# P V products of two key blocks in one group, and projection chunks placed by time, in a fused attention and expert block

## What is computed

```python
xq, xk, xv = x @ wq.T, x @ wk.T, x @ wv.T            # each split into 16 heads
probs = softmax(einsum('bqhd,bkhd->bhqk', xq, xk))   # no scaling
att   = einsum('bhqk,bkhd->bqhd', probs, xv).reshape(4, 1024, 512) @ wo.T
x = layernorm(x + att)
logits = x @ Wr.T + br                               # 8 experts
h = einsum('nd,erd->ner', x, A)                      # all experts, rank 64
y = einsum('ner,eor->neo', h, B) / 64                # the expert of the largest logit, times its softmax
x = layernorm(x + selected y)
```

## Time and profile before

| | us |
|---|---|
| median of 3 timed runs | 1701.31 |
| lowest and highest | 1699.29, 1701.86 |
| the profiled execution | 1692.17 |
| span of its trace | 1690.3 |
| TensorE matmul busy | 1580.4 (94% of the span) |
| GpSimd busy | 1175.7 (70%) |
| VectorE busy | 942.7 (56%) |
| ScalarE busy | 770.5 (46%) |

### The profile page before, as it was taken

The page is one execution under the profiler, slowest core; times in us unless marked ns, Lnnn a source line. Parts: engine busy times, 40 slices in busy tenths (PEclk is TensorE's granted clock), DMA queues, the critical chain, the costliest instruction groups (busy, mean ns, idle before and its releaser), DMA issues.

```text
span 1690.3 us, 19384 instructions
## 1 busy us (share of the span) xinstructions
PE 1580.4 (94%) x6432; PEld 755.5 (45%) x6432; DVE 942.7 (56%) x1688; ACT 770.5 (46%) x1409; POOL 1175.7 (70%) x653
## 2 busy tenths in 40 slices
PE   5979999999999999999999999999999999999897
PEld 2534444444444444444444454444444444444343
DVE  1645556654465566655456555755545676773433
ACT  1144455554445444444444444444544555555322
POOL 1067889987777667667778766686777888889600
PEclk9999999999999999999999999999999999999899
DMA  7343434332032222234331133312423112210001
GB/s 242 95 131 107 151 101 111 103 104 73 10 93 70 76 71 69 56 94 126 94 84 48 40 82 88 82 46 85 141 45 88 45 46 58 57 39 20 7 1 50
DMA packets 82066, 132.08 MB, mean 78 GB/s; under 512 B 18592, under 2 KB 36016, under 8 KB 81968
## 3 DMA queue, kind: packets, MB, share of 16 engines
q1 hardware_dynamic: 78704, 125.59, 26.8%
q0 software_dynamic: 1152, 4.22, 0.7%
q10 hardware_dynamic: 2112, 1.05, 0.2%
HBM read 87.84 MB, written 42.20 MB: 77 GB/s over the span
## 4 chain that ended last, share of the span: by engine, by line
PE 83%; DVE 7%; issue 4%; POOL 3%; ACT 2%; DMA 1%; SPq 1%; ACTq 0%; POOLq 0%
PE sc L547 14%; PE pv L559 13%; PE w L448 13%; PE mx L537 13%; PE w L459 7%; PE w L511 6%; PE w L470 5%; PE w L498 5%; DVE mxc L723 2%; POOL Psum L382 2%; PE w L492 1%; DMA wqk_s<-wkT 1%; DVE eq L804 1%; ACT P L612 1%; PE w L505 1%
## 5 line engine op out<-in xcount | busy, mean ns | idle before, releaser
L723 DVE TENSOR_REDUCE mxc<-mx 128x1 f32<-128x512 f32 x1024 | 685.0, 686 | 589.1 <-PE mx L537 585.9
L382 POOL TENSOR_TENSOR Psum<-Psum,P 128x1024 f32<-128x1024 f32 x384 | 901.9, 2366 | 150.4 <-ACT P L612 146.0
L612 ACT ACTIVATE P<-sc 128x512 f32<-128x512 f32 x1024 | 594.3, 596 | 653.4 <-PE sc L547 644.8
L547 PE MATMUL sc<-stack 98*128 98x512 f32 x1024 | 679.6, 664 | 13.8 <-DMA stack<-mrow 12.0
L537 PE MATMUL mx<-stack 96*128 96x512 f32 x1024 | 412.9, 406 | 6.4 <-DVE mxc L723 6.4
L547 PEld LDWEIGHTS sc<-stack 98*128 98x128 f32 x1024 | 193.4, 189 | 292.5 <-issue 138.5
L378 POOL TENSOR_TENSOR Psum<-P 128x1024 f32<-128x1024 f32 x64 | 151.2, 2369 | 233.5 <-ACT P L612 226.6
L448 PE MATMUL w<-xT_s,wqk_s 128*128 128x512 f32 x512 | 266.6, 613 | 27.2 <-DMA wqk_s<-wkT 17.7
L559 PE MATMUL pv<-P,V 128*32 128x512 f32 x2048 | 273.6, 606 | 0.0
L537 PEld LDWEIGHTS mx<-stack 96*128 96x128 f32 x1024 | 195.5, 191 | 171.8 <-issue 140.8
L448 PEld LDWEIGHTS w<-xT_s,wqk_s 128*128 128x128 f32 x512 | 92.7, 192 | 112.2 <-issue 85.7
(11 more groups left out here) (108 smaller groups left out, 821.6 us busy)
## 6 DMA issues: line engine op xcount, KB each, us to landing
stack<-qk_parts SPq DMA_DIRECT2D x192, 256.0 KB, 5.3
qk_parts<-split SPq DMA_DIRECT2D x64, 512.0 KB, 2.8
xT_s<-xT SPq DMA_DIRECT2D x8, 1024.0 KB, 10.2
den_s<-den_parts SPq DMA_DIRECT2D x124, 64.0 KB, 2.0
r<-x SPq DMA_DIRECT2D x3, 2048.0 KB, 8.6
out<-r SPq DMA_DIRECT2D x12, 512.0 KB, 3.0
wqk_s<-wqT SPq DMA_DIRECT2D x14, 256.0 KB, 4.0
wqk_s<-wkT SPq DMA_DIRECT2D x14, 256.0 KB, 4.3
```

The lines of the kernel that those rows point to most:

```text
L382: pool.tensor_tensor(Psum[:, s % 2, i, :], Psum[:, s % 2, i, :], P[:, unit % NP, :], ALU.add).then_inc(add_done, 1)
L547: pe.matmul(sc[c][:, :], stack(s, i)[0:KS, 0, 128 * kb:128 * kb + 128], stack(s, i)[0:KS, 1, 512 * c:512 * c + 512], start=True, stop=True ...
L612: act.activation(P[:, unit % NP, 512 * c:512 * c + 512], sc[c][:, :], ACT.Exp).then_inc(exp_done, 1)
L723: dve.tensor_reduce(mxc[:, q % 2, m:m + 1], mx[g % NMX][:, :], AX.X, ALU.max).then_inc(mx_done, 1)
```

## The change

Three things are changed.

1. `out_block` becomes `out_group`: the P V matmuls of two key blocks follow one another, eight in a group. There are four groups in a slot: after the max item of h11, h19 and h27, and h3 of the next slot. What waits for `pv_done` counts groups: `exp` of a unit waits for the group that read its P buffer, `copy_v` and `copy_out` likewise. The number of P buffers stays six.
2. The three segments are gone. `paced` walks through the halves with a cost for each (2 for a half, 9 more for a half with a group, 4 for a chunk) and places chunks so that the sum grows evenly. Halves with a group get no chunk, nor mostly does the half behind it. A slot's pieces keep their order.
3. `den` and `max_t` are no longer at fixed halves. They go to the first half from h10 and h26 on in which no piece is half done, and at the latest to h12 and h28 in the middle of a piece. SyncE's `load_max` stands in the half after `max_t`. The steps behind `den` (spread, store, reload, inversion, normalisation) count from h12 instead of h10.

```diff
-    SEGMENTS = ((0, 10), (10, 26), (26, 32))
+    HALF_COST, GROUP_COST = 2, 9
+    DEN_AT, MAX_AT = 10, 26
...
+    def group_of(h):
+        k, c = divmod(h, 2)
+        return k // 4 - 1 if c == 1 and k % 4 == 1 else None
...
+    def paced(pieces, pinned):
+        pieces, pinned = list(pieces), list(pinned)
+        chunks = [(kind, n, c) for kind, n in pieces for c in range(CHUNKS[kind])]
+        cost = [HALF_COST + (GROUP_COST if group_of(h) is not None else 0) for h in range(HALVES)]
+        work = sum(WEIGHT.get(kind, 4) for kind, _, _ in chunks) + sum(WEIGHT[kind] for _, (kind, _) in pinned)
+        each, spent, out = (sum(cost) + work) / HALVES, 0, []
+        for h in range(HALVES):
+            spent += cost[h]
+            out.append([])
+            while pinned and h >= pinned[0][0] and (not chunks or chunks[0][2] == 0 or h >= pinned[0][0] + 2):
+                _, (kind, n) = pinned.pop(0)
+                out[-1].append((kind, n, 0))
+                spent += WEIGHT[kind]
+            while chunks and (h + 1 == HALVES or spent + WEIGHT.get(chunks[0][0], 4) / 2 <= each * (h + 1)):
+                out[-1].append(chunks.pop(0))
+                spent += WEIGHT.get(out[-1][-1][0], 4)
...
         def den_half(s):
-            return HALVES * (s + 1) + SEGMENTS[1][0]
+            return HALVES * (s + 1) + DEN_AT + 2
...
-                if h == SEGMENTS[2][0] + 1 and s < LAST:
-                    load_max(s + 1)
+                for q in ends(half - 1, "max_t"):
+                    load_max(q)
...
-            def out_block(s, kb):
-                pe.wait_ge(exp_done, 2 * (UNITS * s + 2 * kb + 2))
+            def out_group(s, g):
+                pe.wait_ge(exp_done, 2 * (UNITS * s + 4 * g + 4))
...
-                for c in range(2):
-                    for i in range(2):
+                for kb in (2 * g, 2 * g + 1):
+                    for c in range(2):
+                        for i in range(2):
...
-                if c == 1 and k == 1 and s:
-                    out_block(s - 1, KB - 1)
-                if c == 1 and k % 2 == 1 and k >= 3:
-                    out_block(s, (k - 3) // 2)
+                g = group_of(half % HALVES)
+                if g is not None and (g >= 0 or s):
+                    out_group(s if g >= 0 else s - 1, g % GROUPS)
...
-                    act.wait_ge(pv_done, (unit - NP) // 2 + 1)
+                    act.wait_ge(pv_done, (unit - NP) // 4 + 1)
```

More of the change, by code:

```diff
@@ L23, in build_attention_lora_moe_block @@
     KB = S // 128
+    GROUPS = KB // 2
     PAIRS = H // 2
@@ L42, in build_attention_lora_moe_block @@
     CHUNKS = {"qk": KT, "v": KT, "o": KT, "part": KT - 1, "h": KT, "z": KT, "t1": 1, "t2": 1, "lg": 1, "den": 1, "max_t": 1}
-    WEIGHT = {"t1": 2, "t2": 2, "lg": 4, "den": 0, "max_t": 0}
-    SEGMENTS = ((0, 10), (10, 26), (26, 32))
+    WEIGHT = {"t1": 2, "t2": 2, "lg": 4, "den": 4, "max_t": 1}
+    HALF_COST, GROUP_COST = 2, 9
+    DEN_AT, MAX_AT = 10, 26
     def qks(b, first, n):
@@ L104, in build_attention_lora_moe_block @@
     OPENING = qks(0, 0, 4) + tiles("v", 0, 0, 8) + qks(0, 4, 2) + [("max_t", 0)] + qks(0, 6, 2)
+    def group_of(h):
[17 more added lines that the diff above has]
+                spent += WEIGHT.get(out[-1][-1][0], 4)
+                while pinned and h >= pinned[0][0] and (not chunks or chunks[0][2] == 0):
+                    _, (kind, n) = pinned.pop(0)
+                    out[-1].append((kind, n, 0))
+                    spent += WEIGHT[kind]
+        return out
     AT, ENDS = {}, {}
@@ L107, in build_attention_lora_moe_block @@
     for s in range(SLOTS):
[L108 to L119, removed]
+        pinned = ([(DEN_AT, ("den", s - 1))] if s else []) + ([(MAX_AT, ("max_t", s + 1))] if s < LAST else [])
+        for h, chunks in enumerate(paced([piece for part in PLAN[s] for piece in part], pinned)):
+            for kind, n, c in chunks:
+                AT.setdefault(HALVES * s + h, []).append((kind, n, c))
+                if c == 0:
+                    ORDER.append((kind, n))
                 if c + 1 == CHUNKS[kind]:
-                    ENDS.setdefault(half, []).append((kind, n))
-                spent += weight
-            ORDER += pinned + pieces
+                    ENDS.setdefault(HALVES * s + h, []).append((kind, n))
     FIRST = KB * (B - 1)
@@ L348, in _ @@
                 for after, job in ((1, spread_den), (3, store_rec), (4, load_rden)):
-                    if s and h == SEGMENTS[1][0] + after:
+                    if s and half == den_half(s - 1) + after:
                         job(s - 1)
-                if h == SEGMENTS[2][0] + 1 and s < LAST:
-                    load_max(s + 1)
+                for q in ends(half - 1, "max_t"):
+                    load_max(q)
             for g in range(KB // 2):
@@ L548, in score @@
                           stack(s, i)[0:KS, 1, 512 * c:512 * c + 512], start=True, stop=True).then_inc(sc_ready, 1)
-            def out_block(s, kb):
-                pe.wait_ge(exp_done, 2 * (UNITS * s + 2 * kb + 2))
+            def out_group(s, g):
+                pe.wait_ge(exp_done, 2 * (UNITS * s + 4 * g + 4))
                 if s % PAIRS == 0:
-                    pe.wait_ge(v_done, KB * (s // PAIRS) + kb + 1)
-                if kb == 0 and s:
+                    pe.wait_ge(v_done, KB * (s // PAIRS) + 2 * g + 2)
+                if g == 0 and s:
                     pe.wait_ge(pv_copied, s)
-                for c in range(2):
-                    for i in range(2):
[L558 to L561, removed]
+                for kb in (2 * g, 2 * g + 1):
+                    for c in range(2):
+                        for i in range(2):
+                            at, head = HD * (2 * c + i), 2 * (s % PAIRS) + i
+                            done = pe.matmul(pv[at:at + HD, :], V[:, kb, HD * head:HD * head + HD],
+                                             P[:, (UNITS * s + 2 * kb + i) % NP, 512 * c:512 * c + 512],
+                                             start=(kb == 0), stop=(kb == KB - 1))
                 done.then_inc(pv_done, 1)
@@ L587, in _ @@
                     KIND[kind](n, chunk, bank)
-            out_block(LAST, KB - 1)
+            out_group(LAST, GROUPS - 1)
             pe.wait_ge(exp_done, 2 * UNITS * SLOTS)
@@ L622, in copy_v @@
                 if n >= KB:
-                    act.wait_ge(pv_done, KB * (PAIRS * (n // KB) - 1) + n % KB + 1)
+                    act.wait_ge(pv_done, GROUPS * (PAIRS * (n // KB) - 1) + n % KB // 2 + 1)
                 act.activation(V[:, n % KB, :], BANK["v", n][:, :], ACT.Copy).then_inc(v_done, 1)
             def copy_out(s):
-                act.wait_ge(pv_done, KB * (s + 1))
+                act.wait_ge(pv_done, GROUPS * (s + 1))
                 if s > 1:
@@ L859, in _ @@
                     gates(n)
-                if s and h == SEGMENTS[1][0] + 3:
+                if s and half == den_half(s - 1) + 3:
                     reciprocal(s - 1)
```

## The result

The changed kernel takes 1748.19 us (median of 4 runs, 1747.45 to 1750.94), the kernel before, run beside it, 1701.03 us. The ratio is 1.028, with a 95% interval of 1.026 to 1.030. The change makes the kernel 47 us slower, where 1695 us was forecast with a range up to 1710.

What follows compares the result with a forecast made beforehand. TensorE's list was taken as the bound. Gains of 41, 17.6 and 6 us against costs of 15.3, 30.2, 9 and 3.3, plus 1 for the clock, gave -6 us: 1695 us timed, range 1680 to 1710.

Steps and rivals of the forecast that it cites:

- What bounds the kernel: TensorE's list is the bound: busy 94% of the span, with ScalarE and VectorE waiting for it.
- Gain 1: P V matmuls in groups of eight pay the 0.32 us shape-change gap once: 128 times, 41 us saved.
- The rival that gave the gap to every four matmuls: The gap is not the shape change's, so grouping P V matmuls saves 0: 1736 us; chance 0.05.
- Gain 2: At `max_t`, the chunk behind no longer waits for the ended piece's bank in 11 slots: 17.6 us saved.
- Cost 2: At slot starts and in packed slots, chunks wait for banks that VectorE empties late: +30.2 us, between 15 and 36.
- stops overlap: Bank stops and late row maxima share time, packed slots wait half as often: another -15 us, 1680; chance 0.16.
- Gain 3: VectorE's `reciprocal` behind `den` no longer waits for SyncE's spreading DMAs, stopping max items: 6 of 6.4 us saved.
- Cost 1: With `max_t` late, at h28, TensorE waits for row maxima before the next slot's first score: +15.3 us.
- Cost 3: In empty halves behind a group, the third score start waits for ScalarE's Exp: 33 places at 0.27, +9 us.
- Cost 4: In slots 8, 16 and 24 the first output projection waits for GpSimd's later normalisation: +3.3 us.
- At nothing, the P buffers: Six P buffers cost nothing: an `exp` waiting for a group has its own score behind that group on TensorE.
- The rival "the clock": Ten slot starts with bank and row-maxima stops each lose full clock for one stretch: +16 us, 1711; chance 0.17.

Runs made afterwards that it cites:

- e10_max_early: The changed kernel with slot 2's chunks held to h14, free-form gates (tie-break left out) and `max_t` from h24 instead of h26: 1677.8 us, ratio 0.989.

## Why the prediction was wrong, step by step

**What bounds the kernel**: right. TensorE's list stayed the bound.

**Gain 1 (-41)**: right as a price, 0.31 us for each of 128 groups. Wrong as time: the groups alone brought 3 us in the old order, because held gates and the stops and half clock behind them took the rest; with the gates or the bank stops out of the way they brought 28 and 29. The rival that gave the gap to every four matmuls is refuted.

**Gain 2 (-17.6) and Cost 2 (+30.2)**: together +12.6. The bank waits (releasers `split` and `r`, rows above and all smaller ones) sum to 40.4 us before and 54.7 after: +14.3. Right as a sum; but the eleven stops of Gain 2, taken at 1.6 each, measure 13.8 us in the trace of the kernel before and not 17.6, since four of them are under 1 us. The rival "stops overlap" did not come.

**Gain 3 (-6)**: the reduction's wait went from 6.4 to 2.6: -3.8.

**Cost 1 (+15.3)**: the wait for `mrow` went from 12.0 to 26.2: +14.2. Right as a wait. As time it cost more: without it `e10_max_early` is 32 us faster, and half clock followed most of these starts.

**Cost 3 (+9)**: halves that hold a score and a max item alone and take over 0.6 us from mark to mark, with no stop and at full clock, are 22 before and 54 after, and lose 6.4 and 15.8 us: +9.4. Right. **Cost 4 (+3.3)**: 4.1. **At nothing, the P buffers**: right, TensorE's waits for Exp are 0.9 us before and 2.0 after.

**What the sum lacked**: the x load of slot 2 (13.6 where it was 1.4: 12.2), stack loads late on SyncE (3.5), gates that held `hm` (6.7 + 1.2 before, 6.6 + 4.8 after: 3.5), GpSimd ahead of one `den` (1.5), Exp (1.1), 22 us together. The first is a plain miss: each moved chunk's inputs have to be followed to their DMA. The prediction looked at the queue behind the row maxima and not at what a moved chunk reads.

**The clock, the step that failed.** The prediction took 1 us, since slot 20 kept its full clock where slot 12 lost it. The lost clock grew by 44 us. The sum then reads -40 + 14.3 - 3.8 + 14.2 + 9.4 + 4.1 + 22 = +20, and with at most 44 for the clock 64, against 55 measured between the two spans; by difference the clock thus cost some 35 us, an estimate that takes in whatever else the sum has wrong. The rival "the clock" had the right mechanism and was too small. It counted ten starts at 1.7 us, 17 in all. The stretches at eight starts last 41 us together and cost up to 20; another 54 us at half clock lie behind the x load (17), h10's `den` and other stops. Some of these stretches ran on: after the stop at 981.11 of the kernel after, the clock was at half for twice the time that the earlier trace rows shows:

```profile
972.00:980.40 8.40, 6.03 (x20) 3.35 (x20) 6.30 (x13) 3.16 (x7) 4.72 (x2) 1.00 0.16 62
980.40:987.20 6.80, 6.09 (x26) 1.29 (x26) 1.35 (x3) 1.19 (x2) 2.36 (x1) 0.50 0.02 1
```

Of the ten starts eight lost the clock, more than the six from which the rival was to decide. Of the signs set down, the group's 2.52, the 26.2 us for `mrow` in 12 places and a clock below 0.98 (0.966) came as written; the last was the one that would mean wrong. Slots 10 and 18 grew by 4.5 and 7.2 us instead of 3, and slots 13 and 21 shrank by 1.8 and 1.7 instead of 3.

## What to carry to other kernels

A gain on the bound engine is worth its price only where no other engine decides: before counting it, take the list of that engine's stops, and ask which of them stay at the same place on the clock. Stops of 1 to 3 us that come close together cost twice, once as waits and again as half clock, so two stops side by side should be priced as both, and parted before anything else is tuned. And a piece that only writes a bank (a small transpose, a row of sums) is best followed by work that needs none: two halves without chunks were worth 51 us here, more than the 29 of the groups.

## What the runs showed of the hardware

An operation of 8 columns on VectorE, 0.29 us alone, takes up to 2.44 us beside GpSimd's add of 2.37, while a reduction of 512 columns takes its 0.69 in all of 1024 cases (621 to 694 ns). Of the 1024 reductions 426 lie wholly inside a GpSimd add. The form decides it, not the size: with one SBUF input and unlike pitches all 32 gate operations take 0.28 us, and 14 of them lie wholly inside a GpSimd add. The Trainium skill, "SBUF — State Buffer", section "Who interferes with whom", says that VectorE and GpSimd exclude each other for the whole instruction where the VectorE operation runs in a two-port mode, or has two SBUF inputs while GpSimd reads SBUF too. The trace agrees for `eq` (two inputs, 2.14 us). For the old `gate` (one input, 2.42 us) it agrees if that operation ran in such a mode, which no run shows by itself.

At slot 7's start TensorE stood for 2.50 and 1.38 us close together, and the clock fell to 1.2 GHz for 3.4 us of nearly full work; around the stop that ended at 981.11 it was 6.8. Single stops of 1.3 to 1.65 us mostly left it at full: the loop of the kernel before has 19, 15 of them behind `max_t`, and no half clock behind any. Of 23 lone stops of that size in the kernel after, four have one behind them. In the loop there are 2 stretches at half clock before (10 us) and 18 after (102 us). Thirty matmuls in idle time gave 14 to 17 us back.
